# Attention product of exponentials and values: two halves of 375 queries in one stretch every fourth round, in place of a quarter in every round

## What is computed

```python
qm = jnp.einsum('bhsd,dr->bhsr', q, M_U)
km = jnp.einsum('rd,bhtd->bhrt', M_V, k)
attn = jnp.einsum('bhsr,bhrt->bhst', qm, km) * scale
attn = jax.nn.softmax(attn, axis=-1)
out = jnp.einsum('bhst,bhtd->bhsd', attn, v)
```

## Time and profile before

| | |
|---|---|
| median of three runs | 3381.99 us (3378.26 to 3388.05) |
| the profiled execution's own time | 3387.41 us |
| its span | 3385.6 us |
| PE busy | 3120.8 us, 92% of the span |
| DVE busy | 2153.1 us, 64% |
| ACT busy | 1675.6 us, 49% |
| POOL busy | 630.7 us, 19% |
| granted TensorE clock, mean | 0.96 of full speed |

### The profile page before, as it was taken

How to read it: one execution, slowest core, us unless ns; L and a number is a source line. 1 busy time by engine, 2 the same in 40 slices (tenths; PEclk the granted TensorE clock), 3 DMA queues, 4 the chain that set the end, 5 groups by cost and what they waited for, 6 DMA issues and landing times.

```text
span 3385.6 us, 56227 instructions
## 1 busy us (share of the span) xinstructions
PE 3120.8 (92%) x22512; PEld 1795.2 (53%) x22512; DVE 2153.1 (64%) x3828; ACT 1675.6 (49%) x2419; POOL 630.7 (19%) x1097
## 2 busy tenths in 40 slices
PE   6888999999999999998999999999999999999977
PEld 3543455464555546464554646455554646455545
DVE  3317666766766676676767676676667667667635
ACT  1123654646455464646546464645546464655542
POOL 1520130301212030211203030121303021120211
PEclk7667999999999999999999999999999999999989
DMA  5325220312122031312213031222203131221000
GB/s 128 112 88 106 73 53 14 79 29 72 33 63 45 15 89 23 79 23 70 38 40 72 14 79 26 67 41 59 50 15 80 32 77 24 64 38 28 7 8 7
DMA packets 146212, 174.52 MB, mean 52 GB/s; under 512 B 30081, under 2 KB 134874, under 8 KB 143950
## 3 DMA queue, kind: packets, MB, share of 16 engines
q1 hardware_dynamic: 143772, 163.37, 20.1%
q0 software_dynamic: 1280, 7.08, 0.9%
q10 hardware_dynamic: 898, 0.47, 0.1%
HBM read 105.49 MB, written 64.51 MB: 50 GB/s over the span
## 4 chain that ended last, share of the span: by engine, by line
PE 70%; DVE 14%; ACT 7%; issue 4%; SPq 2%; DMA 2%; POOL 1%; ACTq 0%; DVEq 0%; POOLq 0%
PE ps L1118 67%; DVE negm L929 7%; ACT big L746 2%; DVE st L873 2%; ACT hn L709 1%; PE ps L1204 1%; ACT rest L671 1%; PE ps L1292 1%; ACT parts L687 1%; DVE mpart L936 1%; SPq L384 1%; DVE onrm L960 1%; DVE rest L1033 1%; POOL h0t L494 0%; DVE mvr L879 0%
## 5 line engine op out<-in xcount | busy, mean ns | idle before, releaser
L929 DVE TENSOR_REDUCE negm<-ps 125x1 f32<-125x750 f32 x1152 | 1064.2, 935 | 548.4 <-PE ps L1118 536.4
L746 ACT ACTIVATE big<-ps 125x750 f32<-125x750 f32 x1152 | 907.3, 794 | 659.1 <-PE ps L1118 656.2
L1118 PE MATMUL ps<-qs,ks 99*125 99x375 bf16 x2304 | 615.5, 349 | 69.7 <-DVE negm L929 59.1
L1118 PE MATMUL ps<-ks,qs 96*125 96x375 bf16 x2304 | 587.2, 337 | 64.0 <-ACT big L746 28.7
L1118 PE MATMUL ps<-big,V 125*32 125x188 f32 (+1 forms) x9216 | 584.8, 333 | 3.3 <-ACT big L746 0.4
L1033 DVE SCALAR_TENSOR_TENSOR rest<-ps,fb,h1s 128x375 f32<-128x375 f32 (+1 forms) x448 | 251.7, 603 | 322.9 <-PE ps L1118 321.6
L1118 PEld LDWEIGHTS ps<-qs,ks 99*125 99x125 bf16 x2304 | 230.3, 136 | 402.1 <-issue 223.4
L1118 PEld LDWEIGHTS ps<-ks,qs 96*125 96x125 bf16 x2304 | 292.0, 140 | 209.2 <-issue 52.8
L760 ACT ACTIVATE h1s<-ps,fb,wsc 128x375 f32<-128x375 f32 (+1 forms) x448 | 272.4, 658 | 210.6 <-PE ps L1118 210.6
L494 POOL TENSOR_TENSOR h0t<-h0t,onrm 125x384 f32<-125x384 f32 x48 | 48.1, 1002 | 1751.7 <-DVE onrm L960 1751.7
L1118 PEld LDWEIGHTS ps<-big,V 125*32 125x32 f32 x9216 | 195.9, 108 | 298.9 <-issue 285.2
(11 more groups left out here) (176 smaller groups left out, 3250.3 us busy)
## 6 DMA issues: line engine op xcount, KB each, us to landing
qs<-qk_scratch SPq DMA_DIRECT2D x288, 93.8 KB, 3.5
ks<-qk_scratch SPq DMA_DIRECT2D x288, 93.8 KB, 4.5
qk_scratch<-parts SPq DMA_DIRECT2D x32, 562.5 KB, 4.7
v_scratch<-vtmp SPq DMA_DIRECT2D x16, 1125.0 KB
V<-v_scratch SPq DMA_DIRECT2D x48, 375.0 KB
h_scratch<-h0t SPq DMA_DIRECT2D x16, 562.5 KB
hn<-h_scratch SPq DMA_DIRECT2D x16, 562.5 KB
h0t<-h_scratch SPq DMA_DIRECT2D x16, 562.5 KB
```

Source lines behind the costliest of these rows:

```text
L746: nc.scalar.activation(halves(probs[:, i % 2, h, :]), slot(s, TP), ACT.Exp).then_inc(exp_done, 1)
L929: V_.tensor_reduce(negm[:, n:n + 1], slot(s, TP), axis=AX.XY, op=MAX, negate=True).then_inc(max_done, 1)
L1118: return nc.tensor.matmul(o, l, r, start=start, stop=stop)
```

## The change

`PV_COLS` has two entries in place of four, so a part is one half of 375 queries, and a key tile has two parts. A table `PV_AT` names the round after whose tile A a key tile's two parts go out together: round 6 for key tile 0, then 10, 14, 18 and 22 for key tiles 1 to 4. The sixth key tile goes out after tile A of round 1 of the next section (`PV_FIRST`), or in `ffn` as before. There are as many columns to multiply as before, in half as many matmuls: 2304 in place of 4608. No other engine's list of instructions changes, nor do its waits.

```diff
-PV_COLS = ((0, 188), (188, 375), (375, 563), (563, 750))
-PV_FROM = HG + 1
+PV_COLS = ((0, 375), (375, 750))
+PV_AT = {HG * i + HG + 2: (2 * i, 2 * i + 1) for i in range(J - 1)}
+PV_FIRST = {1: (2 * J - 2, 2 * J - 1)}
 PV_LAST = range(len(PV_COLS) * (J - 1), len(PV_COLS) * J)
...
-                    if pending is not None and kind in "AB" and k < 2:
-                        if ("A", k) in tiles:
-                            pv_parts(*pending, (PV_LAST[2 * k + (kind == "B")],))
-                        elif kind == "B":
-                            pv_parts(*pending, PV_LAST[2 * k:2 * k + 2])
-                    if kind == ("A" if ("A", k) in tiles else "B") and k > PV_FROM:
-                        if k == PV_FROM + 1:
-                            pv_parts(b, g, (0,))
-                        pv_parts(b, g, (k - PV_FROM,))
+                    if kind == ("A" if ("A", k) in tiles else "B"):
+                        if pending is not None:
+                            pv_parts(*pending, PV_FIRST.get(k, ()))
+                        pv_parts(b, g, PV_AT.get(k, ()))
...
-                pv_parts(b, g, range(TILES - PV_FROM, PV_LAST[0]))
```

## The result

| | before | changed |
|---|---|---|
| median | 3380.12 us (3364.04 to 3388.05) | 3478.43 us (3472.89 to 3486.18) |
| profiled execution, its span | 3387.41, 3385.6 | 3472.89, 3471.0 |
| granted clock, mean | 0.96 | 0.937 |
| at half clock after 330 us, from the record of the granted clock | 14 intervals, 73.3 us | 54 intervals, 254.1 us |

The changed kernel is slower: ratio 1.0301, interval 1.0278 to 1.0324, 98 us on the medians. The half-clock time leaves out the first 330 us, the start-up, and counts the end. Both forecast (3390) and range (3358 to 3418) missed.

A forecast was written before the change was run, and what follows sets the result against it. It took TensorE as the bound in rounds with a part, and the three-slot tile ring in rounds without. Plain and second sections +5, first +9, third -3.5, the end -3 made +8 us on 3382: 3390, range 3358 to 3418.

The forecast's parts named there:

- Steps (1) and (2): Product stretches on TensorE: two halves take 1.42; 48 fewer separate stretches at 0.28 take 13.6 us per clip off TensorE.
- Step (3): Rounds without a part wait for the ring of three tile slots: four rounds take 5.08 us against 4.96.
- Steps (5) and (6): VectorE and ScalarE side work by section: second sections +0.3 us, first ones +0.6, third ones -0.25.
- Step (7): Last section and end of the one before, rounds with only B: -3 us over some 25 rounds.
- Step (8): Waits on `exp_done` and `pv_done`: neither was or becomes the last to arrive, so no cost.
- rival D: Longer TensorE waits, at most 0.8, could drop the clock to 1.2 GHz; held unlikely, chance 0.19 together with Rival A.
- step (5): Side work on VectorE and ScalarE in a section without anything else costs 2.4 us in place of 1.7.
- Rival A: Side work in the three rounds behind a stretch isn't covered: 0.7 in each of 46 sections, +32, 3422; 0.19 with rival D.

The follow-up runs named there:

- e1: The changed kernel with products of a zero stationary operand on TensorE ahead of tiles that were seen to wait; 3413.64 us, ratio 1.0078.
- e7: The kernel before with the change's places, four quarter parts in one stretch, only in the fourteen third sections that hold projections; 3439.58 us, ratio 1.0176.
- e3: The changed kernel with four quarter parts in each stretch in place of two halves; 3495.63 us, ratio 1.0315.
- e4: The changed kernel with one half after tile A of every second round in place of both halves every fourth; 3392.95 us, ratio 1.0031.
- e5: The kernel before with four chained memsets, about 1.2 us, on VectorE ahead of the splitting of the maxima; 3469.61 us, ratio 1.0237.
- e9: The kernel of e4 unchanged, measured once more for a profile of a typical execution; 3387.91 us.

## Why the prediction was wrong

**Steps (1) and (2)**, the stretch and the switches, held: 1.40 for 1.42, and 189 off PE busy in e1 (48 x 0.28 is 13.4 per clip and 215 in all; the prediction has 13.6 and 217).

**Step (3)**, the ring, held: 5.17 for 5.08. The 0.09 comes from the tile A that I had at 2.11 behind the stretch's B: it follows the B before it, which I had at 1.88, by 0.37, so it can't stand before 2.25; it stands at 2.26 (1477.37 - 1475.11), and the last ones move with it.

**Steps (5) and (6)** were near. In e1, in clips where neither kernel has a fall, first sections are 0.4 and third ones 0.3 longer than before (forecast +0.6 and -0.25). The changed kernel's first sections are 1.9 longer with one fall of 3.4 and 3.4 with two, so such a fall costs about 1.5; its third ones are 2.8 longer with one of 6.8 against an old one without, so that costs 2.5. Its second sections are 2.2 longer with one of 3.4, which leaves +0.7 (forecast +0.3). That is 1.4 per clip for 0.65, some 20 us over fourteen clips for 9. In e1 the second section is +1.5; 0.35 of it is the splitting of the maxima, which took 1.77 there and 1.42 before, and the rest stays unresolved between side work and fillings. **Step (7)** gave -1.0 in the last section and +0.7 in the one before it, together -0.3 for -3. **Step (8)** held: TensorE stood idle for 4.6 us in all ahead of the parts.

**The step that failed is the clock.** The sum had no term for it, and rival D, which set it aside, said that the new waits are at most 0.8 long with work between and called a fall unlikely. Both halves were wrong. The waits where side work meets a bare round are 1.05 (DVE) to 1.7 (ACT), and they recur in every clip; nor would 0.8 have been safe, as the fall behind 0.51 and 0.64 shows. The bound of 0.8 stood there without a row of its own, and the side work that step (5) had just put into these rounds was not added to it. And the row that was to show safety, a busy 10.04 of 12 at clock 1.00, was a sample of one place: the old kernel itself had 14 intervals at half clock, and I never asked its record where they lay or what stood ahead of them. Nine lie at round 2 of third sections, behind waits of 0.64, 0.85 and 0.31, two at round 13 of first ones, behind 0.39 and 1.10, and three at the end.

The extra 181 us at half clock (254.1 - 73.3), at 1.5 for each 3.4, are an estimated 80 us. Added up by sections it is somewhat less: between the profiled executions, 85.4 apart, the 42 sections of the second to the fifteenth clip are 90.8 longer, some 20 of it the sum without the clock as above and some 71 the falls, while the rest of the execution is 5.4 shorter. e1, with the falls filled, has 64 of the 90.8 back. I also gave D no price. Rival A's sign was right, and the wait of over 1 us behind DVE that I had named as its sign is there (1.05), but the same wait is where D's fall begins, so that sign could not tell the two apart; A's mechanism carries at most the 20 of steps (5) and (6), of which 9 were in the forecast, and A had 32 on top.

The page "TensorE: Matmul & The Clock Gate" of the Trainium skill, section "A second HAM failure mode: psum-queue depth-cycling", describes a case like this: a kernel that cycles through PSUM banks idles briefly and often between groups of matmuls, and the clock swings between its two levels. The traces agree, with 54 intervals for 14. Its section "HAM oscillation — how this bites in real kernels" puts the penalty at half of the time at the low level; by that, an estimate, the 181 would cost 90. The pair before and e7 shows 1.6 of 3.4, and a fall of 6.8 cost 2.5.

What stays open is the rule by which a given wait brings a fall. The pairs show that the same wait (1.10, 1.39, 1.69) does in one place or execution and not in another, and some falls have no wait over 0.64 ahead; what else decides was not isolated. The same third sections show it too: with the four quarters in a stretch those of the second to the fourteenth clip have two falls each in e7 and at most one in e3.

## What to carry to other kernels

Before moving TensorE's work into fewer and longer stretches, lay the record of the granted clock over the timeline: where does it fall already, and which waits stand ahead? A change that leaves TensorE's sum of work smaller but lengthens single waits beyond what the kernel had is to be priced with up to a fall per wait, 1.5 us each here; not each wait brings one. Half the merging (one half every second round, e4) with a filling in the one longest wait won 0.35%.

## What the runs showed of the hardware that was not expected

- Superfluous TensorE work can shorten the time: 999 zero products, 214 us of busy time, took 65 us off the changed kernel.
- A clock fall can outlast its cause: in e5 a wait of 1.39 is followed by 13.7 us at 1.2 GHz with TensorE busy for 3.00 of 3.00.
- An edit in one section can slow an untouched one: the first sections of e7, 1.6 each in thirteen clips.
- The four small VectorE instructions that split the maxima (24 columns, all in SBUF) take 0.98 together in e4's second sections and 1.89 in e9's, the same kernel. In both, POOL runs its own instructions of 1.0 us one behind the other at that time (`hn<-hn,mvr,rstd`, 192 columns). The seventh clip in e4:

```profile
L937 DVE CAST mpart<-negm x1: 178/178/178, 1434.7 to 1434.7; 125x24 bf16<-125x24 f32 x1
L938 DVE TENSOR_TENSOR mres<-negm,mpart x1: 183/183/183, 1434.9 to 1434.9; 125x24 f32<-125x24 f32 x1
```

and in e9, with the tile B behind it waiting 1.16 in place of 0.24:

```profile
L937 DVE CAST mpart<-negm x1: 429/429/429, 1444.3 to 1444.3; 125x24 bf16<-125x24 f32 x1
L938 DVE TENSOR_TENSOR mres<-negm,mpart x1: 445/445/445, 1444.8 to 1444.8; 125x24 f32<-125x24 f32 x1
```

It costs 0.9 per second section. The page "SBUF — State Buffer" of the Trainium skill, section "SBUF: two separate sides", says that a VectorE instruction with two SBUF inputs or in a two-port mode and one of GpSimd that reads SBUF exclude each other, for the whole of the one that started first. The traces agree with the sharing and not with the whole: in e4 the CAST and the TENSOR_TENSOR take their 0.18 inside a POOL instruction that runs from 1434.18 to 1435.18. In e9 POOL's instructions start at 1443.74, 1444.73 and 1445.72, and VectorE's four end at 1444.77, 1445.25, 1445.76 and 1446.24, each within 0.04 behind the end of one of POOL's or 0.52 behind a start. By these two traces it matters where in POOL's instruction VectorE's falls; no run moved POOL's work to test it.
